# A two-layer graph kernel: padding put ahead of node 0, and 13 second-stage gathers issued before the row table is complete

## The reference

```python
# layer 0
msg = edge_weight[:, None] * x[src]
nb  = segment_sum(msg, dst)
out = x @ W1.T + b1 + (nb + nb * x) @ W2.T + b2
out = leaky_relu(out, 0.2); out = out / max(norm(out), 1e-12)
x1  = layernorm(x + out)
# layer 1
e   = relu(edge_attr_64 @ ee_w1 + ee_b1) @ ee_w2 + ee_b2
agg = segment_sum(x1[src] + e, dst)
h   = (1 + eps) * x1 + agg
h   = relu(ln(h @ w1 + b1)); h = relu(ln(h @ w2 + b2)); y = h @ w3 + b3   # 256 -> 1024 -> 1024 -> 256
x2  = layernorm(x1 + relu(ln(x1 + y)))
```

## Time and profile before

| what | us |
|---|---|
| median of 3 runs | 1167.76 (1167.53 to 1170.28) |
| span of the profiled execution | 1168.9 |
| its own time beside the span | not given apart; only the span and the three runs are |
| TensorE busy | 1103.3 (94%) |
| VectorE busy | 974.4 (83%) |
| GpSimd busy | 818.6 (70%) |
| ScalarE busy | 628.0 (54%) |

### The profile page before, as it was taken

The page is one execution under the profiler, slowest core; times in us unless marked ns, Lnnn a source line. Parts: engine busy times, 40 slices in busy tenths (PEclk is TensorE's granted clock), DMA queues, the critical chain, the costliest instruction groups (busy, mean ns, idle before and its releaser), DMA issues.

```text
span 1168.9 us, 20816 instructions
## 1 busy us (share of the span) xinstructions
PE 1103.3 (94%) x5279; PEld 901.7 (77%) x5279; DVE 974.4 (83%) x2790; ACT 628.0 (54%) x1526; POOL 818.6 (70%) x855
## 2 busy tenths in 40 slices
PE   6899999999999999998789999999999999999996
PEld 4787777777777677776568888888888888888885
DVE  6899999999999999999677877887787788778865
ACT  4575656666656665665534445444544554455453
POOL 7777777777777777777667767776776777677610
PEclk9899999999999999999699999999999999999999
DMA  7456676676676556656867777777777677777620
GB/s 208 135 166 191 187 206 194 188 206 194 187 202 176 170 169 176 173 165 185 246 185 217 217 210 208 209 216 207 210 213 216 204 210 214 210 210 208 204 75 12
DMA packets 100813, 221.44 MB, mean 189 GB/s; under 512 B 19335, under 2 KB 50945, under 8 KB 100738
## 3 DMA queue, kind: packets, MB, share of 16 engines
q0 software_dynamic: 53408, 164.16, 49.0%
q1 hardware_dynamic: 47330, 56.46, 15.7%
HBM read 203.71 MB, written 16.83 MB: 189 GB/s over the span
## 4 chain that ended last, share of the span: by engine, by line
PE 52%; DVE 14%; POOL 12%; issue 10%; DMA 6%; ACT 3%; SPq 1%; ACTq 0%; DVEq 0%; POOLq 0%
PE ps_z L1154 29%; POOL raw L778 12%; PE ps_s L1111 9%; PE ps_y L1154 6%; DVE msg L1802 4%; DMA raw<-in_x,src_all 4%; PE ps_tr L1221 4%; DVE msg L1808 3%; DVE oh L135 2%; PE ps_e L929 2%; ACT msg L1413 2%; ACT msg L1416 1%; DVE x L1854 1%; PE ps_sum L936 1%; PE ps_sum L934 1%
## 5 line engine op out<-in xcount | busy, mean ns | idle before, releaser
L833 POOL DMA_INDIRECT grow<-table_dram,src_all x410 | 394.2, 961 | 162.5 <-issue 97.6
L778 POOL DMA_INDIRECT raw<-in_x,src_all x399 | 388.6, 974 | 121.6 <-issue 110.9
L1154 PE MATMUL ps_z<-w_high,a 128*128 128x512 f32 x784 | 252.4, 393 | 0.5 <-DVE a L2086 0.5
L934 PE MATMUL ps_sum<-msg,oh 128*128 128x512 f32 x464 | 227.6, 491 | 18.8 <-DVE msg L1808 18.7
L135 DVE TENSOR_SCALAR oh<-lane,rel 128x128 fp32r<-128x128 f32 x919 | 215.3, 297 | 25.9 <-DMA raw<-in_x,src_all 25.6
L929 PE MATMUL ps_e<-we,attr 65*128 65x256 f32 x832 | 224.6, 391 | 10.1 <-DVE msg L1808 6.5
L1413 ACT ACTIVATE msg<-raw,w_sb 128x256 fp32r<-128x256 f32 x416 | 194.2, 500 | 66.2 <-DMA raw<-in_x,src_all 57.2
L929 PEld LDWEIGHTS ps_e<-we,attr 65*128 65x128 f32 x832 | 155.7, 194 | 48.7 <-issue 23.0
L1802 DVE SCALAR_TENSOR_TENSOR msg<-raw,w_sb,msg 128x256 fp32r<-128x256 f32 x416 | 182.5, 476 | 11.2 <-ACT msg L1416 10.0
L936 PE MATMUL ps_sum<-msg,oh 128*128 128x512 f32 x464 | 184.0, 397 | 0.0
L1154 PEld LDWEIGHTS ps_z<-w_high,a 128*128 128x128 f32 x784 | 147.3, 188 | 30.4 <-issue 0.9
(11 more groups left out here) (147 smaller groups left out, 1450.0 us busy)
## 6 DMA issues: line engine op xcount, KB each, us to landing
attr<-in_attrT SPq DMA_DIRECT2D x50, 192.0 KB, 3.5
raw<-in_x,src_all POOLq DMA_INDIRECT x416, 3.0
grow<-table_dram,src_all POOLq DMA_INDIRECT x410, 3.7
table_dram<-table SPq DMA_DIRECT2D x25, 256.0 KB
w_raw<-in_m_w SPq DMA_DIRECT2D x12, 512.0 KB, 5.9
attr<-in_attrT SPq DMA_DIRECT2D x24, 160.0 KB, 3.2
xs<-in_x SPq DMA_DIRECT2D x25, 128.0 KB, 2.3
xTb<-in_xT SPq DMA_DIRECT2D x25, 128.0 KB, 2.6
```

What stands on the lines that cost most here:

```text
L778: pool.indirect_dma_start(out=raw[:, j, :], out_offset=None, in_=x, in_offset=bass.IndirectOffsetOnAxis(ap=src_all[:, q * TILES + j:q * TI ...
L833: pool.indirect_dma_start(out=grow[:, j, :].bitcast(F32), out_offset=None, in_=table_dram, in_offset=bass.IndirectOffsetOnAxis(ap=src_all[ ...
L934: pe.matmul(ps_sum[bank][:, :], oh[:, slot, :], msg[:, j, 0, :], start=start, stop=False, skip_group_check=True)
L1154: mm = pe.matmul(acc, left[a], right[b], start=False, stop=stop and a == 1, skip_group_check=True)
```

## The change

The 75 padding nodes and their 1275 edge places are now ahead of node 0. Block 0 is the short one (53 nodes, tiles 9 to 16), block 24 is whole, and both stages take the blocks in the order 0 to 24. The pairs of tiles are cut as 1, 2, 2, ... instead of 2, 2, ..., 1. Stage 2 begins with block 0 as p = 0; with its eight tiles, the first five of block 1 are gathered early. Indices and one-hots of absent sources are made on DVE at the start of stage 1, counted on PE after block 0 of stage 1, and kept in `counts` through the stage. The early gathers wait for step 3 of block 24 (`summed`) and no longer for its finished sum. SP loads the biases of the dense layers after the last `xs`, between the last table stores.

```diff
-PAIRS = [(0, 2), (2, 2), (4, 2), (6, 2), (8, 2), (10, 2), (12, 2), (14, 2), (16, 1)]
+PAIRS = [(0, 1), (1, 2), (3, 2), (5, 2), (7, 2), (9, 2), (11, 2), (13, 2), (15, 2)]
+EARLY_PAIRS = 3
+EARLY_TILES = FIRST_TILES + EARLY_NEXT
...
     def row_free(self, p, k):
-        if p == 0:
+        if p == 1 and k < FIRST_PAIR:
             return 0
         if k < 2:
             return SUMS * (p - 1) + 2
         if PAIRS[k][0] + PAIRS[k][1] <= TILES - self.edge:
-            return 0 if p == 1 and k >= LAST_PAIRS else SUMS * (p - 1) + k + 1
-        return SUMS if p == 1 else SUMS * p + 1
+            return SUMS * (p - 1) + k + 1
+        return SUMS * p + 1
...
@@ SP, end of stage 1 @@
-                sp.wait_ge(message, NP * (BLOCKS - 1))
-                for layer in range(3):
-                    load_bias(layer)
+                load_xr(BLOCKS - 2)
                 load_xs(BLOCKS - 1)
-                load_xr(BLOCKS - 2)
+                store_table(BLOCKS - 3, 0)
                 load_xT(BLOCKS - 1)
-                store_table(BLOCKS - 3, 0)
+                store_hb(BLOCKS - 3, 0)
                 load_xr(BLOCKS - 1)
-                store_hb(BLOCKS - 3, 0)
+                load_first_hb()
+                load_bias(0)
                 store_table(BLOCKS - 2, 1)
+                load_bias(1)
                 put_table(BLOCKS - 1, 0)
+                load_bias(2)
...
@@ POOL @@
                 def early_gathers():
-                    pool.wait_ge(s_ready, BLOCKS)
+                    pool.wait_ge(early_done, 1)
                     pool.wait_ge(zero_stored, 48)
+                    pool.wait_ge(summed, SUMS * LAST + 4)
                     pool.wait_ge(table_stored, 16 * (BLOCKS - 2))
-                    for j in range(LAST_TILES):
+                    for n in range(EARLY_TILES):
...
                     pool.wait_ge(table_stored, 16 * BLOCKS)
                     pool.wait_ge(edge_dense, BLOCKS)
-                    for j in range(TILES - path.edge, TILES):
-                        row_gather(path, 0, last - 1, j)
                     for p in range(1, BLOCKS):
-                        for j in range(TILES):
-                            row_gather(path, p, block_at(p), j)
-                    for j in range(path.edge):
-                        row_gather(path, BLOCKS, last, j)
+                        for j in range(EARLY_NEXT if p == 1 else 0, TILES):
+                            row_gather(path, p, p, j)
...
@@ PE, start of stage 2 @@
-                    count_sources(path)
-                    first_step(path, 1)
+                    for c in range(FIRST_PAIR, SUMS - 1):
+                        first_step(path, c)
                     pe.wait_ge(prep2, 3)
-                    pe.wait_ge(counts_copied, 1)
                     copy_highs(0, 2)
-                    first_step(path, 2)
+                    add_absent(0)
+                    first_step(path, SUMS - 1)
                     pe.wait_ge(dd_end[-1], DD)
                     copy_highs(2, 5)
-                    add_absent()
-                    first_step(path, 3)
-                    copy_highs(5, 8)
-                    first_step(path, 0)
                     turn_h(path, 0)
-                    copy_highs(8, 13)
+                    copy_highs(5, 13)
...
-                    sums(path, 1, 0, 2)
+                    sums(path, 1, 0, EARLY_PAIRS)
+                    add_absent(1)
...
@@ PE, stage 1 @@
+                near_block(path, 0, 0)
+                count_sources(path)
...
@@ DVE, stage 1 @@
+                for c in range(FIRST_PAIR, FIRST_PAIR + LEAD):
+                    near_oh(path, 0, c)
+                early_sources()
+                for k in range(FIRST_PAIR, FIRST_PAIR + LEAD):
+                    messages(0, k)
...
+            LAST_BLOCK_TAILS = {0: (2, range(2, 7)), 1: (2, range(7, 10)), 2: (2, range(10, DD + 1)), 4: (1, range(1, 2)),
+                                5: (1, range(2, 7))}
+            def near_last_block(path, b, bank):
+                for k in range(LEAD, NP):
+                    s = k - LEAD
+                    follow(b, k)
+                    near_oh(path, b, k)
+                    messages(b, k)
+                    if s == 1:
+                        take_s(b - 1, SUMS * b, 1 - bank)
+                    if s in LAST_BLOCK_TAILS:
+                        back, steps = LAST_BLOCK_TAILS[s]
+                        for n in steps:
+                            tail(b - back, n, (b - back) % 2)
...
@@ DVE, start of stage 2 @@
-                    weight_lows_from_copies(0, 8)
-                    take_h(0, SUMS, 0)
-                    weight_lows_from_copies(8, 10)
+                    weight_lows_from_copies(0, 2)
+                    take_h(0, SUMS)
+                    weight_lows_from_copies(2, 4)
                     h_low(0)
-                    weight_lows_from_copies(10, 13)
+                    near_oh(path, 1, 0)
+                    near_oh(path, 1, 1)
+                    near_oh(path, 1, 2)
+                    weight_lows_from_copies(4, 13)
                     stats(0, 0, 0)
...
@@ ACT, after block 0 of stage 1 @@
+                act.wait_ge(counted, 1)
+                act.wait_ge(bias0_ready, 2)
+                act.activation(counts[:, :, :].rearrange("p b n -> p (b n)"), ps_w[:, :], ACT.Copy)\
+                   .then_inc(counts_copied, 1)
...
-        "x": pad(a["x"], (ROWS_PADDED, D)),
+        "x": a["x"], "x_rows": pad(a["x"], (ROWS_PADDED, D)),
```

548 lines of the change are left out of this document (277 added, 271 removed).

## The result

The changed kernel takes 1177.70 us (median of 4 runs, 1177.28 to 1178.54), the kernel before 1168.24 in the same comparison: ratio 1.0088, 95% interval 1.0071 to 1.0104. It is slower by 9.5 us. The prediction had 1166.5, with a range from 1162.5 to 1170.5.

The account below looks back on a forecast made before the run. Source gathers on POOL were taken to bound stage 1, PE stage 2, with a chain over several engines between. Terms 0.3 - 4.6 + 1.8 + 1.4 - 0.24 = -1.3 from 1167.76 gave 1166.5 us, range 1162.5 to 1170.5.

Parts of the forecast that it names:

- (a): Stage 1: new early DVE work lengthens a few source gathers; +0.3 us, between 0 and 1.2.
- R2: Rival: the ring of `raw` stalls early in stage 1 for 5 us, giving 1171.5 us; chance 0.10.
- (b): Change of stages: block 24's sum 4.1 us earlier, at 543.6; early gathers start near 538 and leave the chain.
- (c): First block of stage 2: ACT's wait goes, high part of h at about 559.5 instead of 568.45, 9 us earlier.
- (d): DVE's work from h's low part to the second statistics; POOL's release moves from 586.02 to 581.4, -4.6 us.
- (e): POOL's restart: one sum instruction instead of four, but 20 gathers instead of 18 to go; together +1.8 us.
- (f): PE's clock behind the restart may fall while PE waits for rows; +1.4 us, between 0 and 3.2.
- POOL's idle time before the restart: Sign in the changed profile: over 15 us, ending with the first sum of p = 1.
- R3: Rival: PE's copies and ACT's weights bound the first block, early gathers don't matter; +3.2, 1171 us; chance 0.07.
- R1: Rival: clock stays high and DVE's chain is at its best; -4.0, 1163.7 us; chance 0.34.
- (g): Stage 2: one tile less, so one PE matmul less; -0.24 us.

Follow-up runs that it names:

- b00: The kernel before, unchanged, run again for a second profile; 1165.20 us.
- e9: Changed kernel with the table instruction moved between the next message's halves and the single-tile message made edge part first; 1169.04 us, ratio to before 1.0014.
- e1: Changed kernel with the table instruction moved behind the edge part of the single-tile message, instead of between its halves; 1171.39 us, ratio to before 1.0042.

## Why the prediction was wrong

**Step (a), the length of stage 1, failed.** It had +0.3 and a bound of 1.2, since only the early DVE work was counted as new; the stage grew by 9.84 us (545.23 against 535.39). The sentence that the new pairs "leave their spacing to POOL" is the error: the count of gathers and the length of a free one don't change with the cut, but the DVE instructions that stand over their starts do. A sign of it was in the rows: the earlier trace rows has gathers of 0.94 and 1.03, and the prediction took the 0.09 for a thing of DVE's load, to be multiplied by 13 new instructions. It is a thing of single instructions at single places: in the ten profiles of the faster chips all 200 source gathers of 1.15 us or more from 60 us on begin while a DVE instruction with two SBUF inputs is under way. No term of the sum and none of the rivals had it. R2 looked for a stall of the ring; POOL's waits for messages (L807) are 6.4 us in all in the changed kernel and were 10.7 before (L778), none over 0.3 us.

**Step (b) was right that gathers leave the chain, and wrong on the sum.** Block 24's sum comes at +12.7 after the last source gather, not at +8.2. `xs` of block 24 is issued at 544.90, right behind the sum of block 23, with no bias ahead of it. The biases were not what bound the sum before: what ended DVE's last wait there was PE's sum, as it is after the change (0.69 and 0.72 us). When the last gather goes, DVE has the messages of four pairs and the tails of two blocks ahead, not three and one. The early gathers start at 550.91 and not near 538: they wait 5.68 us for block 22's table, which the new order of the last block makes behind the sum of block 23. "Its table is ready by 535" was a wrong reading of the profile of before: the table made at 534.48 is block 21's, and that of block 22 was made 0.5 us ahead of its store, so the biases hadn't held that store either. DVE of the kernel before:

```profile
545.46 0.42 DVE L1860 TENSOR_TENSOR table<-tb,table 128x256 fp32r<-128x256 f32 x1
...
546.90 0.42 DVE L1818 SCALAR_TENSOR_TENSOR s_r<-xs,ps_sum 128x256 f32<-128x256 f32 x1 [0.69 <-PE ps_sum L936]
```

**Step (c) held in kind.** ACT's wait ahead of the high part of h (4.61 us in the earlier trace rows) is gone, as forecast:

```profile
572.42 0.36 ACT L1542 ACTIVATE hT<-ps_tr 128x256 fp32r<-128x256 f32 x1
```

The low part of h is at +27.6; by step (d), which has it at 559.7, it would be at +24.3. The 7.1 us gained against the profile of before (10.4 forecast) lack about what (b) had wrong.

**Step (d) held:** 9.67 us from the low part of h to the second statistics, where 9.0 to 10.8 was forecast. The way from the low part of h to the second statistics is 5.8 us longer than before, and that eats most of the 7.1 us. The first sum of p = 1 then comes 3.4 us sooner than in the first profile of before, where -4.6 was forecast. Not all of that is the change: PE's sixteen matmuls of layer 2 took 5.82 us in that profile, where the granted clock was 0.50 from 580 to 584 us, and 3.89 in the changed one at 1.00. Against b00 nothing is gained (+47.1 and +47.2).

**Steps (e) and (f) were too large together.** From the first sum of p = 1 to PE's last wait it is 29.2 us instead of 27.8, 1.4 more, where they had 3.2. Which of the two was too large the profiles don't part. POOL's idle time before the restart was 8.4 and not 15, as the early gathers were late. The clock fell only at the very end of the stretch:

```profile
608.00:612.00 4.00, 4.00 (x22) 1.00 0.72 208
620.00:624.00 4.00, 2.84 (x11) 0.63 0.74 209
```

**The rivals.** R3 (early gathers that don't matter) is out: the low part of h moved by 5 to 7 us. R1 (a clock that stays high, a gain of 4) was right on the clock until the last 2 us of the stretch, but the gain of 4 did not come: in the stretch behind POOL's restart the kernel before had that clock too, 1.00 from 588 us on.

**The sum of (b) to (g)** was -1.6. It measured -3.0 against the profile the prediction was built on (6.8 of span less 9.84) and +1.1 against b00 (12.3 of span less 11.2), and e9, which has stage 1 repaired, is at +0.14% against timed runs. That -1.6 lies between them is luck, as its parts were off both ways. The profile of before had a mean granted clock of 0.87 in the 80 us behind its last source gather, which is some 21 us at half clock, and b00 0.96, some 6 us; PE's last wait came 4.4 us later in the first. A gain reckoned against the first profile was partly the clock's.

## What to carry to other kernels

Where a row of gathers issued by GpSimd is the bound, the length of one is not a constant: look at which VectorE instructions with both inputs in SBUF stand over their starts, and try another place for those beside the longest. A change of tile grouping moves all of them at once, so compare the distribution of gather durations and not only waits; unchanged waits with more busy time is how this showed on the page here. And before pricing a stretch where the clock is low, look at a second profile of the same kernel.

## What the runs showed of the hardware

A source gather here takes 0.95 us when nothing is in the way. Where a DVE instruction with two SBUF inputs was under way at its start it mostly took longer, up to about the start of DVE's next instruction (e1: `msg` from 437.26, next DVE instruction from 437.66; gather from 437.48, 1.08). Not always: in the ten profiles of the faster chips 199 of 908 such gathers from 60 us on stayed below 0.97, 509 took up to 1.15 and 200 more. Of 2812 gathers that began beside none, 2761 stayed below 0.97 and the longest took 1.08. The table instruction behind such a `msg` made the gather 1.42, which is longer by just the 0.34 us to the next instruction of DVE. A memset or an instruction with one input in PSUM in its place did not, and neither did a second `msg`, `y` or `tb` at the same distance (100 gathers of 1.07 to 1.11).

The Trainium skill ("SBUF — State Buffer", section "Who interferes with whom") says that a DVE instruction with two SBUF inputs contends with a GpSimd instruction that reads SBUF, and, outside DVE's two-port modes, not one with at most one SBUF input. These runs agree in the main, with 0.13 us for one and 0.47 where the gather waited for two.

What no run here shows is why a gather waits for the table instruction too and not for the others in its place, and why the kernel before, with the table instruction also right behind a two-input `msg` and over the start of a gather (447.68 against 447.56), pays only 0.08. The order in which the two engines asked may be the reason; it is not tested.
